# Saving the attention stage's input to DRAM batch by batch, inside the stage that produces it

## The reference

```python
# --- layer 0: unshared 3x3 convolution, batch norm, relu
x = x + _L0_conv_ref(_gn(x), ...)
# --- layer 1: deformable 3x3 convolution
x = x + _L1_conv_ref(_gn(x), ...)
# --- layer 2: spatial attention mask, norm of the two regions, gamma and beta maps
x = x + _L2_conv_ref(_gn(x), ...)
# --- layer 3: linear attention along all C*H*W = 65536 positions
x = x + _L3_conv_ref(_gn(x), ...)

def _L2_conv_ref(x, ...):
    ...
    mask = jnp.broadcast_to(mask, x.shape)
    rn_x = region_norm(x * mask, mask) + region_norm(x * (1.0 - mask), 1.0 - mask)
    return rn_x * (1.0 + gamma) + beta

def _L3_conv_ref(x, ...):
    qkv = in_proj_weight[None] * x[:, None, :, :, :, None] + in_proj_bias[None]
    ...                       # q, k pass softplus
    s = jnp.cumsum(k[:, :, :, None] * v[:, :, None, :], axis=1)
    z = jnp.cumsum(k, axis=1)
    y = numer / denom         # q times s, and q times z
    y = jnp.concatenate([jnp.ones_like(y[:, :1]), y[:, :-1]], axis=1)
    y = jnp.sum(hid_proj_weight[None] * y[:, None], axis=-1) + hid_proj_bias[None]
    y = jnp.sum(out_proj_weight[None] * jnp.tanh(y), axis=1) + out_proj_bias[None]
```

## Time and profile before

| | |
|---|---|
| Median of 3 timed executions | 3493.6 us (3492.67 to 3494.13) |
| Profiled execution, own time | 3487.4 us |
| its span (first to last instruction) | 3485.6 us |
| VectorE busy | 1815.1 us (52%) |
| GpSimd busy | 1754.7 us (50%) |
| TensorE busy | 1637.2 us (47%) |
| ScalarE busy | 761.0 us (22%) |
| Granted TensorE clock, mean | 0.722 of full |

### The profile page before, as it was taken

How to read it: one execution, slowest core, us unless ns; L and a number is a source line. 1 busy time by engine, 2 the same in 40 slices (tenths; PEclk the granted TensorE clock), 3 DMA queues, 4 the chain that set the end, 5 groups by cost and what they waited for, 6 DMA issues and landing times. The chain is left out here.

```text
span 3485.6 us, 32244 instructions
## 1 busy us (share of the span) xinstructions
PE 1637.2 (47%) x12432; PEld 974.3 (28%) x12432; DVE 1815.1 (52%) x1717; ACT 761.0 (22%) x893; POOL 1754.7 (50%) x1342
## 2 busy tenths in 40 slices
PE   3666321321313123141231412634888878888887
PEld 2455210110101001010010100431455445445545
DVE  3222432441616326153262534555888887788885
ACT  3111211101102011010111100523433432343341
POOL 0000067576675757757577574044355445535542
PEclk9878655665656556565565655776989999998999
DMA  7999533232332323323233232221131122113212
GB/s 315 431 431 432 234 92 102 71 107 86 95 104 72 108 78 103 103 71 109 77 104 103 72 109 65 85 78 38 58 108 65 57 81 90 57 57 105 67 55 82
DMA packets 118313, 414.64 MB, mean 119 GB/s; under 512 B 24802, under 2 KB 59764, under 8 KB 101108
## 3 DMA queue, kind: packets, MB, share of 16 engines
q1 hardware_dynamic: 62964, 262.86, 19.9%
q0 software_dynamic: 55296, 151.07, 14.1%
HBM read 396.78 MB, written 17.05 MB: 119 GB/s over the span
## 5 line engine op out<-in xcount | busy, mean ns | idle before, releaser
L441 POOL DMA_INDIRECT gath<-table,idx x1152 | 1162.4, 1009 | 561.0 <-issue 347.3
L568 DVE TENSOR_TENSOR gath<-gath,p_stat 128x2304 f32<-128x2304 f32 x128 | 326.4, 2550 | 749.0 <-DMA gath<-table,idx 260.0
L646 PE MATMUL p_col<-ident,taps 128*128 128x128 f32 x512 | 116.4, 367 | 705.8 <-issue 533.8
L495 ACT ACTIVATE cols<-p_col 128x512 f32<-128x512 f32 x128 | 75.2, 597 | 1240.5 <-remote 827.8
L646 PEld LDWEIGHTS p_col<-ident,taps 128*128 128x128 f32 x512 | 77.8, 184 | 751.7 <-issue 744.5
L1251 PE MATMUL p_state<-xt,tri 128*128 128x512 f32 x512 | 257.4, 650 | 64.5 <-DVE prod L1139 64.5
L1019 POOL TENSOR_TENSOR query<-query,expo 128x2048 f32<-128x2048 f32 x16 | 102.1, 6382 | 334.7 <-DVE query L1117 334.7
L1139 DVE TENSOR_TENSOR prod<-p_state,query 128x2048 f32<-128x2048 f32 x80 | 183.0, 2288 | 127.5 <-PE p_state L1256 127.5
L595 PE MATMUL p_conv<-sides,wconv 128*32 128x512 f32 x192 | 70.4, 893 | 330.7 <-ACT rows L466 330.7
L1287 PE MATMUL p_sum<-ident,prod 128*128 128x128 f32 x1024 | 174.0, 341 | 104.0 <-DVE prod L1161 104.0
L1161 DVE TENSOR_TENSOR prod<-hidw,y 128x2048 f32<-128x2048 f32 x64 | 209.1, 3286 | 6.0 <-DMA hidw<-in_hidw 4.3
(11 more groups left out here) (231 smaller groups left out, 2917.4 us busy)
## 6 DMA issues: line engine op xcount, KB each, us to landing
ring<-in_w SPq DMA_DIRECT2D x64, 2304.0 KB, 18.6
hidw<-in_hidw SPq DMA_DIRECT2D x64, 1024.0 KB, 4.9
gath<-table,idx POOLq DMA_INDIRECT x1152
table<-pix SPq DMA_DIRECT2D x64, 128.0 KB, 2.2
xt<-in_x SPq DMA_DIRECT2D x1, 4096.0 KB, 12.5
ring<-in_x SPq DMA_DIRECT2D x1, 4096.0 KB, 12.2
resid<-xt SPq DMA_DIRECT2D x32, 128.0 KB, 2.4
xlate<-resid SPq DMA_DIRECT2D x16, 256.0 KB, 3.0
```

Of the source, the lines that this page charges most:

```text
L441: nc.gpsimd.indirect_dma_start(out=gath[:, t % SLOTS, k].rearrange("p n c -> p (n c)"), out_offset=None, in_=tables[u], in_offset=bass.Ind ...
L568: tt(g, g, w, ALU.mult).then_inc(weighted, 1)
L646: last = nc.tensor.transpose(p_col[t % 2][:, k], taps[:, t, 2 * k:2 * k + 2].rearrange("p k c -> p (k c)"), ident[:])
```

## The change

Stage three's SP list gets, after its seven loads, a loop over the batches: wait until the batch is done, then issue its two copies to `resid`. After the last batch it issues the tiny copy. The same 33 copies leave the head of stage four's SP list. The DRAM tensor and the semaphore `saved` are created outside both stages and handed in. Nothing else changes; the lines behind the first insertion move by five or six.

```diff
-def layer2(nc, xt, d, early, row_stats):
+def layer2(nc, xt, d, early, row_stats, resid, saved):
...
             tiles, early_in = early
             for name, tile in tiles.items():
                 sp.dma_start(tile[:], d[name][:]).then_inc(early_in, 16)
+            rows = resid[:, 0:C * H * W].rearrange("b (c h x) -> b h c x", h=2, x=HALF)
+            for b in range(B):
+                sp.wait_ge(batch_done, b + 1)
+                for h in range(2):
+                    sp.dma_start(rows[b, h], xt[h * C:(h + 1) * C, b]).then_inc(saved, 16)
+            sp.dma_start(resid[:, C * H * W:C * H * W + 2].rearrange("b (o l) -> o b l", o=1), xt[0:1, :, 0:2]).then_inc(saved, 16)
...
-def layer3(nc, xt, d, out, early, row_stats):
+def layer3(nc, xt, d, out, early, row_stats, resid, saved):
...
-        resid = nc.dram_tensor("resid", (B, C * H * W + HALF), F32, kind="Internal").ap()
...
-        saved = sem("saved"); x_in = sem("x_in"); late_in = sem("late_in"); out_done = sem("out_done")
+        x_in = sem("x_in"); late_in = sem("late_in"); out_done = sem("out_done")
...
             sp.dma_start(gnmat[:], d["gnmat"][:]).then_inc(gnmat_in, 16)
-            for b in range(B):
-                for h in range(2):
-                    sp.dma_start(rows[b, h], xt[h * C:(h + 1) * C, b]).then_inc(saved, 16)
-            sp.dma_start(resid[:, C * H * W:C * H * W + 2].rearrange("b (o l) -> o b l", o=1), xt[0:1, :, 0:2]).then_inc(saved, 16)
             for name, tile in (("ident", ident), ("tri", tri), ("pick", pick), ("give", give), ("edge", edge),
...
             early = early_tiles(nc, ctx)
-            layer2(nc, xt, d, early, row_stats)
-            layer3(nc, xt, d, out, early, row_stats)
+            resid = nc.dram_tensor("resid", (B, C * H * W + HALF), F32, kind="Internal").ap()
+            saved = ctx.enter_context(nc.semaphore("saved"))
+            layer2(nc, xt, d, early, row_stats, resid, saved)
+            layer3(nc, xt, d, out, early, row_stats, resid, saved)
```

## The result

| | before | after |
|---|---|---|
| Median of timed executions (11 each; the first three of before are those that the forecast started from) | 3491.17 us | 3469.63 us |
| Ratio after to before | | 0.9949, 95% interval 0.9934 to 0.9963 |
| Profiled execution, own time | 3487.4 us | 3477.76 us |
| its span | 3485.6 us | 3475.9 us |

The change makes the kernel faster by 0.51%, which is 17.8 us of 3491.17, with an interval from 12.9 to 23.0 us. The two medians themselves differ by 21.5 us, which lies in that interval too. The forecast was 19.9 us and 3473.7 us; the measured median lies in the forecast range.

The account below looks back on a forecast made before the run. SP's issue order at stage four's head, copies before constants, was taken as the bound; -21.1 + 1.2 = -19.9 us took the median from 3493.6 to 3473.7 us, 0.57% less, range 3467 to 3480.

Parts of the forecast that it names:

- The copies were on the path, and the constants are late next: Stage four's head: 33 issues ahead of `ident` go, 21.1 us gained in full; `p_turn` still waits for the constants.
- The barrier's term: End of stage three: SP arrives last after three issues, 1.87 us, so the barrier opens 1.2 us later (bounds 0.3 to 2.8).
- the bound that I gave, over 0.4 us: Sign for rival A: more than 0.4 us between SP's last copy and `gnmat`.
- rival A: Stage boundary: SP, last, must fetch its list or empty its queue; opening 1.8 to 2.4 us later, 3475.5 to 3476.1; chance 0.08.
- The closing loop: Stage three's loop: SP keeps up with batches of 3.43 us, and the copies' transfers, some 76 GB/s, cost zero.
- Rival B: Closing loop: transfers stretch the chain by GpSimd's stage-four factor 1.78, adding 40 us, 3514 us; chance 0.03.
- The constants: Stage four, `ident` to `p_turn`: the eight constants take the same 12.8 us after the change.
- rival C: Stage four's constants slow down by more than 12.9 us, so no measurable change, 3487 to 3500 us; chance 0.03.
- TensorE's wait for `outb`: At `p_turn` in stage four: the wait falls to about 10.5 us in place of 30.4.
- The clock: TensorE meets its low clock again at `p_turn`; 3 us either way allowed over stage four's 16 batches.

Follow-up runs that it names:

- kernels with the constants first: Kernel before with eight constants issued ahead of the 33 copies in stage four: ratio 0.9988; with VectorE's wait also moved to its first write over `xt`: 0.9942.
- SP last and no DMA: Kernel before plus SP's wait for VectorE's last statistics at the end of stage three; 0.42 us from their end to `gnmat`, no timed ratio given.
- doubled copies: Changed kernel with each batch's copies issued twice in stage three's loop, the second time to an unread DRAM tensor; ratio 0.9934 to the kernel before.
- last batch late: Changed kernel with the last batch's two copies and the tiny one behind stage four's constants, VectorE's wait at its first write over `xt`; ratio 0.9935.
- early constants: Changed kernel with the eight constants loaded at the start of stage three; 3224.07 us, ratio 0.9918 to the kernel before (3250.99 us there).
- early constants with last batch late: Changed kernel with constants loaded in stage three and the last batch's copies in stage four; 3224.29 us, ratio 0.9915; timed again 3465.45 us, 0.9929.

## Why the prediction was right

The prediction's sum against the traces, from two of the kernel before and three of the changed one:

| step | forecast | measured (means) |
|---|---|---|
| copies leave the stretch `gnmat` to `ident` | -21.1 | -21.1 (21.48 and 21.54, now 0.40) |
| the barrier opens later | +1.2 | +1.4 (1.68, now 3.11) |
| `ident` to `p_turn` | 0 | -0.9 (12.40, now 11.52) |
| last write of `xt` to `value` | -19.9 | -20.6 (36.84, now 16.28) |

**The copies were on the path, and the constants are late next.** Right: the whole 21.1 us came off, and `p_turn` still waits for `outb`. The kernels with the constants first show it from the other side: the copies may stay in stage four if nothing waits for them, and `value` then comes 16.95 us behind the last write, against 15.62 to 16.84 in the changed kernel.

**The barrier's term.** Its mechanism was right, the size was short by a quarter of a us. SP's last three issues ended 1.77 us after the last write, less than the forecast 1.87 (2331.82 to 2333.59), and the opening took 0.65 us and not 0.26. By the bound that I gave, over 0.4 us, this would count for rival A. But that rival's price was 1.8 to 2.4 us, and the barrier opened at 2334.2, before the last copy, issued at 2333.00, could land with its 1.9 us (and the same in this trace), so the queue need not be empty; with SP last and no DMA the delay is 0.16 us. At the price that it was given rival A is refuted, and its bound was set too close: a delay of its kind is there, 0.39 us (0.65 less 0.26). The sentence of the Trainium skill weighed with it (Runtime: NRT & Kernel Launch, instruction fetch mechanics) finds no stall of the size of the rival's price here. Whether a fetch is part of the 0.39 us, no run shows.

**The closing loop** keeps its pitch and durations with single and with doubled copies. Rival B's factor of 1.78 in stage four goes with VectorE's multiplies, as the prediction held against it: 3.31 us beside one while 15 GB/s moved, 1.27 us beside none while 209 GB/s moved. That the doubled transfers left all durations alone agrees with the Trainium skill (SBUF — State Buffer, section on the two separate sides).

**The constants** were taken as fixed at 12.8 us. They scatter from 10.9 to 12.8 with nothing behind them. So the mean of -0.9 is within their scatter and no effect of the change that these traces could show, and rival C, constants that slow down after the change, didn't happen.

**TensorE's wait for `outb`** was forecast at 10.5 us and is 7.3. I had taken the whole 19.9 us from 30.4. But the barrier's delay moves the start of that wait too, so only the 21.1 us come off, and in this trace the constants gave 2.0 more: 30.4 - 21.1 - 2.0 = 7.3.

**The clock** was at its low level at `p_turn` again: it took 1.11 us in both kernels, at a granted clock of 0.50 in both, where a later `p_turn` of the changed kernel at clock 1.00 (start 2465.67) took 0.60 us. From `value` to the end all traces of the two kernels lie between 1128.1 and 1129.2 us, so the 3 us allowed for it weren't needed. What the range did need was room for stage two, of which the prediction had said nothing but that two medians may differ. The measured median is 4.1 us below the forecast one. Of these 2.4 us are the kernel before, whose median went from 3493.6 us of three executions to 3491.17 of eleven, and 0.7 us are the stretch; the rest is within what stage two scatters. So that the stretch came out as forecast is the sum's merit, and that the median fell into a range 13 us wide is partly luck.

## What to carry to other kernels

When an idle engine's queue appears on the chain at a stage boundary, look at the order of its issues: copies whose only purpose is to free memory can go while the data is made, and the loads that the next stage waits for come first. A barrier turns the last issues of a busy queue into a wait for all engines, so the last batch's share may cost more than its place behind the boundary. Here it cost 1.4 us, which came back only in the kernels whose constants had left that queue as well. Read a gain of some 20 us in a kernel of 3500 from the stretch that it changes, between two instructions on either side, and not from the difference of two spans.

## What the runs showed of the hardware

Stage two decides most of what the runs scatter by. The last statistics of stage two start between 2175 and 2207 us in ten traces, and between 1952 and 1955 us in the other four, those of doubled copies, last batch late, early constants and the first of early constants with last batch late, which ran together on one chip. Eight of the ten others ran on two other chips (of the first two traces the chip isn't known), so chip and occasion can't be told apart here. There the kernel before had a median of 3250.99 us, and not 3491 to 3493 us as beside all other kernels. GpSimd's gathers show where most of it is: 216 of the 246 us between the two traces below (183 idle, 33 busy). Their group in the kernel with doubled copies (busy us, mean ns, idle before and its releasers):

```profile
L441 POOL DMA_INDIRECT gath<-table,idx x1152 | 1131.6, 982 | 382.6 <-issue 350.9 <-DMA table<-pix 31.7
```

and in the changed kernel, on the first occasion:

```profile
L441 POOL DMA_INDIRECT gath<-table,idx x1152 | 1164.8, 1011 | 565.7 <-issue 347.0 <-DMA table<-pix 217.3 <-DVE taps L575 1.5
```

The last term is GpSimd's wait for the pixel tables on their way to DRAM: eight or nine waits, 189 to 217 us together, in the ten traces, and a single one of about 31.7 us in the four. What makes the other waits come and go wasn't tried. The gain doesn't hang on it: the versions with `value` at 16 to 19 us behind the last write gave ratios of 0.9934 and 0.9935 in the group of four, and 0.9942 to 0.9949 in the other.
